# A local transformer inside a gated cross-attention stack: round and layer loops written out, weight parts sent in earlier rounds

## The chip, the cores and the metric

The program runs on one core of one Trainium2 chip. The core's engines are TensorE (PE; its weight loads are shown apart, as PEld), VectorE (DVE), ScalarE (ACT), GpSimd (POOL) and SyncE (SP, which issues the DMAs here). The metric is the device time of one execution in microseconds (us); lower is better.

## The reference, cut to what matters

An activation of 16 sequences x 128 tokens x 128 channels passes four gated cross-attentions, each followed by a gated feed-forward network. The first of these networks is a local transformer of its own, six layers deep. It takes two thirds of the time and is what the change touches:

```python
for i in range(DEPTH):      # 6 layers
    x = attn_layer(shift_tokens(x), Wqkv[i], q_scale[i], k_scale[i], Wo[i]) + x
    x = ffn_layer(shift_tokens(x), ln_g[i], ln_b[i], W1[i], b1[i], W2[i], b2[i]) + x

# attn_layer: 16 heads of 64 channels; l2-normalised and rotated queries and keys;
# each token sees its own window of 32 tokens and the one before it
# ffn_layer: layer norm, 128 -> 2 x 341 channels, a * gelu(gate), 341 -> 128
```

## The kernel before

A unit is one sequence (128 tokens) in one layer, so the local transformer has 6 x 16 = 96 units. The units are pipelined four deep. In round n every engine works on part `a` of unit n, part `b` of unit n-1, part `c` of unit n-2 and part `d` of unit n-3. `stages(a, b, c, d)` is one round; each engine has its own, with its instructions in an order written out by hand, and the engines meet through semaphores alone. Layer l's unit n follows layer l-1's unit 15 without a pause, so in a layer's first three rounds some parts still belong to the layer before. There are two sets of buffers for units (`s`, the unit's parity) and two sets of layer weights (`lw[p]`, `qk_scale[p]`, with p the parity of the layer). The first PE instruction of a round is the transpose in `tokens_T`, line L860; the times of rounds below are cut at its starts.

`local_transformer` drives PE, ACT, DVE and POOL. For each layer it writes out rounds 0 to 3, runs rounds 4 to 13 in a hardware loop of five trips with two rounds in each (L515), and writes out rounds 14 and 15. Layer 0 comes first, then a hardware loop of two trips (L525), each with an odd and an even layer (1 and 2, then 3 and 4), then layer 5. In a loop, the count that an instruction waits for is worked out in registers. In rounds 14 and 15 of layers 0 to 4, PE multiplies the next layer's value and output weights together (`values_outputs`, matmuls L1002, which read `wvT` and `wout` in the buffer `moe1_gu` and count `l_wvo_ps`), and POOL makes the next layer's rotary tables ahead of round 14.

SP is driven by `layer_and_next_weights`: its rounds within a layer were written out already, its layer pairs are a loop (L618). Its `stages` issues, in this order:

```python
if c: middle_values0(*c)              # L583: 4 DMAs, after ACT has copied the values; PE needs them a round later
if d: shifted_tokens(*d)              # L595: 1 DMA, after DVE's first residual (l_y1, L2274); DVE's L2278 waits for it
if c: middle_values1(*c, edge=edge)   # L591: 4 DMAs
```

A unit's `c` and `d` on SP belong to work that the other engines do as `a`, `b` and `c`: SP's stage n runs during the others' round n-1. Behind its stage SP sends weights for layers to come: four value parts (256 KB each, to `wvT` and `wout`) and, in layers 1 to 4, eight layer parts (`wqk`, the feed-forward weights, columns, scales) into the other set of `lw`. One part goes behind each stage, beginning with n = 3. Ahead of the first stand two waits: for `l_wvo_ps` (the products that read `wvT` and `wout`), and for `ffn_done`, the count of second residuals (DVE, L2308), which says that the last unit of the layer before is through, so that its weights can be written over.

Of the kernel before, what the change touches and what calls it, by code (L numbers as in the profile page):

```python
# [23 lines left out]
IT = B // G  # L24
DEPTH, LH, LD = 6, 16, 64
# [48 lines left out]
def program(nc, dram, out):  # L74
# [6 lines left out]
    with ctx:  # L81
# [409 lines left out]
        def layer_unit(p, lp, n):  # L491

            if n >= 0:
                return (n % G, At(p, lp, n // G))
            if p:
                return (n % G, At(0, lp, IT + n // G))
            return None if isinstance(lp, int) and lp == 0 else (n % G, At(1, lp - 1, IT + n // G))

        def local_transformer(engine, stages, prepare=None, fresh=False, drain=None):

            def rounds(p, lp, lo, hi, last=True):
                for n in range(lo, hi):
                    four = (layer_unit(p, lp, n - k) for k in range(4))
                    if fresh and not last:
                        stages(*four, fresh=(1 - p, lp + p, n - lo))
                    else:  # L510
                        stages(*four)

            def layer(p, lp, last):
                rounds(p, lp, 0, 4)
                with engine.Fori(2, IT - 1) as pr:  # L515
                    stages((0, At(p, lp, pr)), (1, At(p, lp, pr - 1)), (0, At(p, lp, pr - 1)), (1, At(p, lp, pr - 2)))
                    stages((1, At(p, lp, pr)), (0, At(p, lp, pr)), (1, At(p, lp, pr - 1)), (0, At(p, lp, pr - 1)))
                if prepare and not last:
                    prepare(1 - p, lp + p)
                rounds(p, lp, B - G, B, last)  # L520

            if prepare:
                prepare(0, 0)
            layer(0, 0, False)
            with engine.Fori(0, DEPTH // 2 - 1) as lp:  # L525
                layer(1, lp, False)
                layer(0, lp + 1, False)
            layer(1, DEPTH // 2 - 1, True)
            for n in range(B, B + 3):
                stages(*(layer_unit(1, DEPTH // 2 - 1, n - k) if n - k < B else None for k in range(4)))  # L530
                if drain and n == B + 1: drain()
# [5 lines left out]
        def _(sp):  # L537
# [14 lines left out]
            def layer_parts(p, l):  # L552

                rows = dram["wqk"][l, :, :]
                parts = [[(wqk[p][:, at:at + 512], rows[:, at:at + 512])] for at in range(0, 2 * INNER, 512)]
                parts += [
                    [(wff1[p], dram["wff1"][l, :, :])],
                    [(wff2[p][:, 0:2, :], dram["wff2"][l, 0:256, :].rearrange("(c p) n -> p c n", p=128)),
                     (wff2[p][0:HID - 256, 2, :], dram["wff2"][l, 256:HID, :])],
                    [(lcol[p][:, :], dram["lcol"][l, :, :]), (bff2[p], dram["bff2"][bass.ds(l, 1), :].partition_broadcast(S))],  # L560
                    [(qk_scale[p][:, 0, :], dram["q_scale"][bass.ds(l, 1), :].partition_broadcast(S)),
                     (qk_scale[p][:, 1, :], dram["k_scale"][bass.ds(l, 1), :].partition_broadcast(S))],
                ]
                return parts

            def value_parts(l):

                return [(dst[:, c:c + 4, :], dram[name][l, :, c:c + 4, :]) for dst, name in ((wvT, "wvT"), (wout, "wout")) for c in (0, 4)]
# [28 lines left out]
            def stages(a, b, c, d):  # L597
                edge = a is None or d is None
                if c: middle_values0(*c)
                if d: shifted_tokens(*d)  # L600
                if c: middle_values1(*c, edge=edge)

            def layer_and_next_weights(p, lp, fresh):

                parts = [[(part, wv_loaded)] for part in value_parts(2 * lp + p + 1)]
                if fresh:
                    parts += [[(move, lw_loaded[1 - p]) for move in part] for part in layer_parts(1 - p, 2 * lp + p + 1)]
                for n in range(B):
                    stages(*(layer_unit(p, lp, n - k) for k in range(4)))
                    if n == 3:  # L610
                        sp.wait_ge(l_wvo_ps, 2 * (2 * lp + p + 1))
                        sp.wait_ge(ffn_done, G + (2 * lp + p) * B)
                    if 3 <= n < 3 + len(parts):
                        for (dst, src), done in parts[n - 3]:
                            sp.dma_start(dst, src).then_inc(done, 16)

            layer_and_next_weights(0, 0, False)
            with sp.Fori(0, DEPTH // 2 - 1) as lp:  # L618
                layer_and_next_weights(1, lp, True)
                layer_and_next_weights(0, lp + 1, True)  # L620
            for n in range(B + 3):
# [64 lines left out]
        def _(pe):  # L686
# [556 lines left out]
            for half in range(2):  # L1243
                values_outputs(0, 0, half)
            pe.wait_ge(t_prep, 1)
            local_transformer(pe, stages, fresh=True, drain=first_value_rows)
            attention(XA[1])
            pe.wait_ge(w1_loaded, 128)
# [10 lines left out]
        def _(act):  # L1259
# [376 lines left out]
            for half in range(2):  # L1636
                values_outputs(0, 0, half)
            local_transformer(act, stages, fresh=True, drain=first_value_rows)
            act.wait_ge(w1_loaded, 112)
            attention(XA[1])  # L1640
# [9 lines left out]
        def _(pool):  # L1650
# [241 lines left out]
            for s in range(G):  # L1892
                pool.wait_ge(x_updated, G + LNY)
                pool.memset(xsT[s][:, 0:1], 0.0)
                pool.memset(ysh[s][:, D:D + 64], 0.0).then_inc(v_ones, 1)
            quad_inverse_stds([3])
            local_transformer(pool, stages, rotary_factors)
            attention(XA[1])
            for q in range(QUADS):
# [764 lines left out]
```

## Time and profile before

| | before |
|---|---|
| median of 3 runs | 2504.11 us (2498.87 to 2506.43) |
| profiled execution | 2502.32 us, span 2500.4 us |
| PE busy | 2379.8 us, 95% of the span |
| DVE, ACT, POOL busy | 1861.0, 1770.3, 1662.9 us (74%, 71%, 67%) |
| local transformer, rounds 0 to 95 | 131.5 to some 1767.5 us |
| mean granted PE clock | 0.981 |

A timeline row gives the start, the time taken, engine, line, operation, output and inputs, the number of instructions merged into it, and in brackets the engine's idle time just before it with what ended it. SPq and PEldq are instructions of the sequencer of SP and of PE: issues, register work, branches. A row of a stretch gives its bounds and length, each engine's busy time with its number of instructions, the granted PE clock (1.00 is 2.4 GHz), the DMA share and the GB/s moved. "issue" stands for a wait that no semaphore of the profile explains.

### The profile page before, as it was taken

Reading aid. Unit: us, or ns where it says so; the run is one execution under the profiler, and the core shown is the slowest. Engines: PE = TensorE matmul, PEld = TensorE weight load, DVE = VectorE, ACT = ScalarE, POOL = GpSimd, SP = SyncE. Lnnn points to the kernel's source line nnn. Section 1 sums busy time; section 2 is a strip of 40 time slices with the busy share of each in tenths; the row PEclk is TensorE's granted clock in tenths of the full one; section 3 lists DMA queues with packets and bytes.
Section 4 is the critical chain, followed back from the end, with each engine's and each line's share of the span. In section 5 each row is a group of like instructions: output and inputs, shape, how many; then the busy total and the mean of one; then the engine's idle time right before and its main releaser. Section 6 shows DMA issues by size and latency. Waiting matters only on the chain. (4 is left out here: it accounts for less than half of the span.)

```text
span 2500.4 us, 84963 instructions
## 1 busy us (share of the span) xinstructions
PE 2379.8 (95%) x32650; PEld 1666.1 (67%) x32650; DVE 1861.0 (74%) x4616; ACT 1770.3 (71%) x3859; POOL 1662.9 (67%) x2011
## 2 busy tenths in 40 slices
PE   8889999999999999999999999999889898999898
PEld 6746666566666666566666666666468777999567
DVE  6768887888878887788778878888387776555574
ACT  5668888888878887888878888888653375332555
POOL 5668888888888887788888888888341164000562
PEclk9989999999999999999999999999999998999899
DMA  3011111121111111221121112111350000000022
GB/s 132 2 36 41 34 33 37 48 52 46 32 48 50 47 36 33 55 54 36 34 55 44 48 36 53 33 32 37 89 172 1 1 2 1 1 0 1 20 68 84
DMA packets 98410, 104.07 MB, mean 42 GB/s; under 512 B 34873, under 2 KB 60548, under 8 KB 97540
## 3 DMA queue, kind: packets, MB, share of 16 engines
q1 hardware_dynamic: 98180, 100.93, 15.2%
q8 instruction: 154, 2.52, 0.4%
q14 instruction: 76, 0.62, 0.1%
HBM read 41.31 MB, written 6.09 MB: 19 GB/s over the span
## 5 line engine op out<-in xcount | busy, mean ns | idle before, releaser
L1261 ACT ACTIVATE area<-ps 64x128 f32<-64x128 f32 (+7 forms) x1480 | 747.0, 530 | 201.2 <-PE ps L860 64.8
L1761 POOL TENSOR_TENSOR area<-area 128x512 f32<-128x512 f32 x384 | 485.7, 1275 | 128.5 <-DVE area L2239 120.9
L1776 POOL TENSOR_TENSOR area<-area,rnq 128x512 f32<-128x512 f32 x384 | 397.2, 1045 | 15.3 <-ACT rnq L1434 8.3
L870 PE MATMUL ps<-lw,area 128*128 128x512 f32 x768 | 375.4, 611 | 4.5 <-DVE area L2239 3.2
L898 PE MATMUL ps<-lw,area 128*64 128x512 f32 x1536 | 373.0, 606 | 0.1
L2237 DVE TENSOR_TENSOR area<-ps,table 128x512 f32<-128x512 f32 x384 | 261.3, 681 | 16.9 <-ACT area L1398 16.8
L2219 DVE TENSOR_REDUCE ssq<-area 128x8 f32<-128x512 f32 x384 | 259.6, 676 | 2.1 <-ACT area L1398 2.1
L2239 DVE TENSOR_TENSOR area<-ps,table 128x512 f32<-128x512 f32 x384 | 259.9, 677 | 0.0
L887 PE MATMUL ps<-ident,area 128*128 128x128 f32 x1536 | 237.7, 278 | 5.0 <-POOL area L1776 4.8
L1398 ACT ACTIVATE area<-ps 128x512 f32<-128x512 f32 x384 | 216.8, 590 | 29.3 <-PE ps L870 29.2
L887 PEld LDWEIGHTS ps<-ident,area 128*128 128x128 f32 x1536 | 178.7, 141 | 78.3 <-issue 57.0
L1528 ACT ACTIVATE area<-ps 128x256 f32<-128x256 f32 x208 | 79.2, 384 | 202.2 <-PE ps L1074 202.1
L953 PEld LDWEIGHTS ps<-area 128*32 128x32 f32 x6144 | 156.2, 110 | 90.6 <-issue 63.3
L1784 POOL TENSOR_TENSOR area<-area,mx 128x512 f32<-128x512 f32 x192 | 200.3, 1043 | 22.1 <-DVE mx L2256 21.4
L953 PE MATMUL ps<-area 128*32 128x128 f32 x6144 | 207.9, 276 | 1.5 <-ACT area L1261 1.5
L870 PEld LDWEIGHTS ps<-lw,area 128*128 128x128 f32 x768 | 131.4, 191 | 108.9 <-issue 93.7
L1792 POOL TENSOR_TENSOR area<-area,rc 128x512 f32<-128x512 f32 x192 | 200.0, 1042 | 2.6 <-DVE rc L2270 2.4
L925 PEld LDWEIGHTS ps<-area 64*32 64x32 f32 x12288 | 134.0, 105 | 90.6 <-issue 79.3
L898 PEld LDWEIGHTS ps<-lw,area 128*64 128x64 f32 x1536 | 92.9, 136 | 144.1 <-issue 111.0
L971 PEld LDWEIGHTS ps<-xnT,lw 128*128 128x128 f32 (+1 forms) x1152 | 147.1, 182 | 47.0 <-issue 45.0
L925 PE MATMUL ps<-area 64*32 64x64 f32 x12288 | 164.9, 224 | 1.6 <-ACT area L1261 1.6
L971 PE MATMUL ps<-xnT,lw 128*128 128x128 f32 (+1 forms) x1152 | 162.4, 278 | 0.6 <-ACT xnT L1261 0.6
(290 smaller groups left out, 4950.9 us busy)
## 6 DMA issues: line engine op xcount, KB each, us to landing
area<-area SPq DMA_DIRECT2D x768, 64.0 KB, 2.0
lw<-in_wqk SPq DMA_DIRECT2D x24, 256.0 KB
area<-in_moe_w SPq DMA_DIRECT2D x24, 256.0 KB, 2.8
area<-product_rows SPq DMA_DIRECT2D x16, 256.0 KB
moe_gu<-in_wvT SPq DMA_DIRECT2D x12, 256.0 KB, 3.0
moe_gu<-in_wout SPq DMA_DIRECT2D x12, 256.0 KB, 3.0
area<-area SPq DMA_DIRECT2D x96, 31.8 KB
product_rows<-lw SPq DMA_DIRECT2D x7, 308.0 KB
```

Source lines behind the costliest of these rows:

```text
L870: nc.tensor.matmul(banks[:, lb_qk[j], :], xsT[s], wqk[w.p][:, j * 512:(j + 1) * 512], start=True, stop=True).then_inc(l_qk_ps, 1)
L887: last = nc.tensor.transpose(banks[:, lb_qkT[j], c * S:(c + 1) * S], QR[s][:, j * 512 + c * 128:j * 512 + (c + 1) * 128], ident[:, :])
L898: last = nc.tensor.matmul(banks[64 * odd:64 * odd + 64, lb_v[j], :].rearrange("p (c n) -> p c n", n=D), xsT[s][:, 64 * near:64 * near + 64 ...
L925: last = nc.tensor.matmul(banks[out_rows, lb_scores[m][odd], c * 64:(c + 1) * 64].rearrange("p (b n) -> p b n", n=WINDOW), QKT[s][64 * odd ...
L953: last = nc.tensor.matmul(banks[32 * n:32 * n + 32, lb_att, 0:D], LPT[s][:, at:at + 32], v, start=(c == 0), stop=(c == 7))
L971: last = nc.tensor.matmul(banks[0:hi - lo, lb_up[value], c * S:(c + 1) * S], wff1[w.p][:, at:at + hi - lo], xnT[s][:, :], start=True, stop ...
L1261: return nc.scalar.activation(dst, src, ACT.Identity if kw else ACT.Copy, **kw)
L1761: pool.tensor_tensor(QR[s][:, cols], QR[s][:, cols], RA[s][:, cols], ALU.add).then_inc(l_rsum, 1)
L1776: pool.tensor_tensor(rows, rows, rnq[s][:, 8 * j:8 * j + 8, None].to_broadcast([S, 8, LD]), ALU.mult).then_inc(l_qkn, 1)
L2219: V.tensor_reduce(ssq[s][:, 8 * j:8 * j + 8], blk(SQ[s], j), AX.X, ALU.add).then_inc(l_ss, 1)
L2237: V.tensor_tensor(blk(RA[s], j), src, factors[:, 0:1, :].to_broadcast([S, 8, LD]), ALU.mult)
L2239: V.tensor_tensor(blk(QR[s], j).rearrange("p h (k e) -> p h k e", k=2), other, factors[:, 1:2, :].to_broadcast([S, 8, LD]).rearrange("p h ...
```

## The change

Two things change, with no arithmetic touched. First, all hardware loops of `local_transformer` and SP's loop over layer pairs become Python loops: the 96 rounds (and the three that drain the pipeline) stand one after the other in each engine's program, and every wait is for a constant. Second, SP begins to send parts behind stage 0 instead of stage 3. The wait for `l_wvo_ps` goes with it to n = 0; the wait for `ffn_done` stands at n = 4, ahead of the first layer part.

```diff
             def layer(p, lp, last):
                 rounds(p, lp, 0, 4)
-                with engine.Fori(2, IT - 1) as pr:
+                for pr in range(2, IT - 1):
                     stages((0, At(p, lp, pr)), (1, At(p, lp, pr - 1)), (0, At(p, lp, pr - 1)), (1, At(p, lp, pr - 2)))
                     stages((1, At(p, lp, pr)), (0, At(p, lp, pr)), (1, At(p, lp, pr - 1)), (0, At(p, lp, pr - 1)))
...
             layer(0, 0, False)
-            with engine.Fori(0, DEPTH // 2 - 1) as lp:
+            for lp in range(DEPTH // 2 - 1):
                 layer(1, lp, False)
                 layer(0, lp + 1, False)
...
                 for n in range(B):
                     stages(*(layer_unit(p, lp, n - k) for k in range(4)))
-                    if n == 3:
+                    if n == 0:
                         sp.wait_ge(l_wvo_ps, 2 * (2 * lp + p + 1))
+                    if n == 4:
                         sp.wait_ge(ffn_done, G + (2 * lp + p) * B)
-                    if 3 <= n < 3 + len(parts):
-                        for (dst, src), done in parts[n - 3]:
+                    if n < len(parts):
+                        for (dst, src), done in parts[n]:
                             sp.dma_start(dst, src).then_inc(done, 16)
 
             layer_and_next_weights(0, 0, False)
-            with sp.Fori(0, DEPTH // 2 - 1) as lp:
+            for lp in range(DEPTH // 2 - 1):
                 layer_and_next_weights(1, lp, True)
                 layer_and_next_weights(0, lp + 1, True)
```

## Rows read from the trace of the kernel before

**Rows 1.** Busy time by stretch: the local transformer whole, with the columns.
```profile
core 0: us, PE busy (x) PEld busy (x) DVE busy (x) ACT busy (x) POOL busy (x), PEclk, DMA share, GB/s
131.50:1767.50 1636.00, 1600.69 (x25034) 1003.55 (x25036) 1312.97 (x2962) 1340.46 (x2798) 1367.46 (x1466) 1.00 0.17 42
```

**Rows 2.** Busy time by stretch: round 3 of layers 0 to 5, one row each.
```profile
182.30:198.74 16.44, 16.44 (x265) 10.35 (x260) 13.62 (x31) 13.86 (x29) 14.51 (x16) 1.00 0.20 52
451.14:470.41 19.27, 16.74 (x266) 10.29 (x261) 13.63 (x31) 13.86 (x29) 14.22 (x16) 1.00 0.26 68
723.14:741.77 18.63, 16.73 (x265) 10.28 (x260) 13.64 (x31) 13.87 (x29) 14.20 (x16) 1.00 0.26 70
999.61:1019.11 19.50, 16.80 (x266) 10.34 (x261) 13.63 (x31) 13.91 (x29) 14.20 (x16) 1.00 0.26 66
1271.81:1290.44 18.63, 16.74 (x267) 10.28 (x261) 13.64 (x31) 13.86 (x29) 14.22 (x16) 1.00 0.26 70
1542.98:1559.41 16.43, 16.43 (x265) 10.36 (x260) 13.59 (x31) 13.86 (x29) 14.20 (x16) 1.00 0.15 36
```

**Rows 3.** Timeline of PE in round 3 of layer 1, its two idle times.
```profile
458.66 1.12 PE L870 MATMUL ps<-lw,area 128*128 128x512 f32 x2 [1.08 <-DVE area L2239]
...
461.90 0.66 PE L939 MATMUL ps<-ident,area 128*128 128x128 f32 x4 [1.45 <-POOL area L1792]
```

**Rows 4.** Timeline of DVE at the start of that round.
```profile
449.19 0.29 DVE L2308 TENSOR_TENSOR Y<-ps,area 128x128 f32<-128x128 f32 x1 [0.19 <-PE ps L985]
...
456.78 0.29 DVE L2278 BATCH_NORM_STATS2 st<-area 128x6 f32<-128x128 f32 x1 [4.12 <-DMA area<-area]
```

**Rows 5.** Timeline of SP's issues, stages 3 and 4 of layer 1.
```profile
434.49 2.77 SPq L591 DMA_DIRECT2D area<-area  x4
449.67 0.38 SPq L615 DMA_DIRECT2D moe_gu<-in_wvT  x1
450.21 3.01 SPq L583 DMA_DIRECT2D area<-area  x4
453.35 0.66 SPq L595 DMA_DIRECT2D area<-area  x1
```

**Rows 6.** Waits of SP's queue over the whole span: total, times, longest.
```profile
SPq L615 <- DVE Y L2308: 48.2, 4, 12.1
```

**Rows 7.** Timeline of SP's issues, stages 0 and 1 of layer 1.
```profile
383.68 2.86 SPq L591 DMA_DIRECT2D area<-area  x4
395.77 2.41 SPq L583 DMA_DIRECT2D area<-area  x4
```

**Rows 8.** Timeline of PE in round 15 of layer 0.
```profile
392.07 1.16 PE L1002 MATMUL ps<-moe_gu 64*128 64x128 f32 x16
```

**Rows 9.** Busy time by stretch: rounds 15 and 0, layers 0/1, then 2/3.
```profile
383.58:401.09 17.51, 17.51 (x282) 11.31 (x277) 13.59 (x31) 14.84 (x31) 14.23 (x16) 1.00 0.15 35
401.09:417.92 16.83, 16.53 (x266) 10.42 (x260) 13.67 (x31) 13.86 (x29) 13.87 (x16) 1.00 0.15 35
926.90:948.68 21.78, 17.64 (x283) 11.32 (x277) 15.80 (x33) 14.85 (x31) 16.11 (x18) 0.99 0.15 35
948.68:966.39 17.71, 17.71 (x260) 11.68 (x260) 12.52 (x29) 13.74 (x29) 11.75 (x14) 0.91 0.12 29
```

**Rows 10.** Instructions of line L525 (outer loop): duration min/median/max in ns.
```profile
L525 PEldq COMPARE_BRANCH  x2: 76/2116/4157, 944.3 to 1493.0; - x2
```

**Rows 11.** Instructions of line L515 (inner loop), the same columns.
```profile
L515 PEldq COMPARE_BRANCH  x30: 76/208/242, 231.9 to 1725.3; - x30
```

**Rows 12.** Busy time by stretch: rounds 1-2 of layers 1, 5; rounds 4-13 of 5.
```profile
417.92:451.14 33.22, 32.93 (x526) 20.73 (x520) 27.26 (x62) 27.72 (x58) 28.41 (x31) 1.00 0.13 31
1509.84:1542.98 33.14, 32.90 (x526) 20.73 (x522) 27.18 (x62) 27.72 (x58) 28.40 (x31) 1.00 0.25 68
1559.41:1725.47 166.06, 165.14 (x2607) 104.03 (x2600) 136.27 (x310) 138.62 (x290) 141.99 (x151) 1.00 0.14 34
```

**Rows 13.** DMA queues of the page: kind, packets, MB, share of 16 engines.
```profile
q8 instruction: 154, 2.52, 0.4%
```

## The prediction

> **What bounds the kernel now.** I began with the share of busy time: over the local transformer PE works 1600.7 of 1636.0 us, 98% [rows 1]. DVE, ACT and POOL have about a sixth of their time free. So the pace is PE's, and what can be won here without taking matmuls away is at most PE's idle time of 35.3 us plus whatever stretches its matmuls. I then cut the stretch at the first PE instruction of each round, which gives 96 rounds to compare. An undisturbed round takes 16.4 to 16.8 us, odd and even ones in turn: layer 5's round 3 takes 16.43 us with PE busy throughout [rows 2]. The rounds that stand out are few: round 3 of layers 1 to 4 [rows 2], the step between the two trips of the outer loop [rows 9], and rounds 13 to 15 of layers 0 to 4, which do extra work (rotary tables on POOL, 16 extra matmuls on PE [rows 8]) that the change leaves where it is.
>
> **Round 3.** Layers 1 to 4 take 19.27, 18.63, 19.50 and 18.63 us there, layer 0 takes 16.44 and layer 5 16.43 [rows 2]. The number of instructions on each engine is the same; what is added is idle time, on PE 1.08 us behind DVE and 1.45 us behind POOL [rows 3]. Going backwards: DVE stood 4.12 us waiting for the shift DMA [rows 4]. SP issued that DMA (L595) at 453.35 us. It had ended stage 3 at 437.26 us and issued nothing until 449.67 us, 0.2 us after the second residual of DVE (449.19 + 0.29) [rows 4, 5]; in the queue's own list of waits it is the weight part that waited for L2308, 4 times, 48.2 us [rows 6]. Queued behind this wait were the weight part, four value copies (L583, 3.01 us of issuing) and then the shift. The value copies could have been issued in the 12 us of standstill. So the `ffn_done` wait at n = 3 delays the shift by about the 3.7 us from 449.67 to 453.35 us. It happens in exactly the four layers that have a previous layer to wait for.
>
> With the change SP meets this wait at n = 4, behind the shift DMA of stage 4. That DMA itself waits for DVE's first residual of round 3 (L2274), which stands behind the second residual of round 2 in DVE's own order. When SP comes to the new wait it is therefore satisfied and holds nothing back. The first DMA behind it is a layer part, 0.38 us of issue, in a place where parts stood before. I expect all four rounds to fall to layer 5's 16.43: 2.84 + 2.20 + 3.07 + 2.20 = 10.3 us. The ends of the range: 0 if something else then arrives last, 10.3 if nothing does. I take 10.3.
>
> **The wait moved to n = 0.** `l_wvo_ps` is counted by the matmuls L1002 in round 15, which end at 393.23 us [rows 8]. SP has ended stage 0 at 386.54 and its next issue is at 395.77 us, held by ACT's copy [rows 7]. The wait ends 2.5 us ahead of that, and a part takes 0.38 us to issue [rows 5]. So nothing behind it is issued late: not the value copies of stage 1, nor the shift behind those. The 256 KB then move ahead of the copies. If the copies land 3 us later for it (the size of the queue's whole delay above), PE still needs them only in the middle of the next round, some 12 us after. Cost 0, cover more than 9 us. Parts 1 to 3 and the eight layer parts go behind stages 1 to 11, places equal to those that stages 4 to 14 had. The last part lands some three rounds earlier; POOL's tables before round 14 did not wait for it before, so no gain.
>
> **The outer loop.** Rounds 15 and 0 take 17.51 + 16.83 = 34.34 us between layers 0 and 1, and 21.78 + 17.71 = 39.49 us where the outer loop branches back [rows 9]. The branch on PE's sequencer took 4157 ns there and 76 ns where it falls through [rows 10]. The second part of the loss is 0.9 us in the round after: no PE idle, but the granted clock has a mean of 0.91, that is, part of it at 1.2 instead of 2.4 GHz, after an idle of 4.1 us. Written out, both go: 39.49 - 34.34 = 5.15 us. DVE, ACT and POOL lose less at their own branches and are not the pace. The Trainium skill has this rule in "Runtime: NRT & Kernel Launch", section "Instruction fetch mechanics": a taken branch to a page that is not in the instruction buffer waits for a DMA fetch. The trace agrees, with 4157 ns.
>
> **The inner loops.** Of 30 branches on PE, 24 are taken, at some 208 ns each [rows 11]. If each showed in full on PE the gain would be 24 x 0.208 = 5.0 us. But PE's idle time is no larger in the loop: layer 5 is busy 165.14 of 166.06 us over ten loop rounds, idle 0.92, and busy 32.90 of 33.14 in two written ones, idle 0.24, or 1.20 for ten [rows 12]. The branch only takes the place of a wait for POOL that the written rounds have. What is left is the difference of the totals: 166.06 - 5 x 33.14 = 0.36 us a layer, 2.2 us for six. Written rounds of layers 1 to 4 still use registers for the layer: 33.22 for two rounds against 33.14 in layer 5 [rows 12]. With rounds 0 and 3 alike that is 0.16 us a layer, 0.6 us for four. Sum 2.8, bounds 0 and 5.0 + 0.6 = 5.6.
>
> The Trainium skill puts a compare-and-branch at some 108 ns ("Advanced Engine Details and Errata", section "Control Flow Timing"). The trace has nearly twice that on PE [rows 11]; by the page 24 branches would be an estimated 2.6 us.
>
> **What is added: a longer program.** Written out, the body is 99 rounds of instructions instead of 4 x 8 + 3 = 35. PE runs some 526 matmuls in two rounds [rows 12], as many weight loads, and 24 repeated trips were served without a new fetch: 24 x 2 x 526 = 25,200 instructions. Its queue brought 154 packets, 2.52 MB, so 16.4 KB each [rows 13]; PE's other 40,000 instructions over 154 packets are some 260 a packet. That makes about 97 more packets. Do they cost time? Layer 5's rounds 1 to 3 are written out, are fetched as they run, and are the fastest of all; round 3 has no PE idle at all [rows 2, 12]. So 0; the bound above follows with the rivals.
>
> **Sum.** 10.3 + 5.15 + 2.8 = 18.3 us, 0.7%. The profiled execution's span of 2500.4 becomes 2482.1, and its own time 2502.3 becomes 2484.0. It lay 1.8 us below the median of the runs, 2504.1, so I predict a median of 2485.8, rounded to 2486. About 0.3%, 7.5 us, can be told from no change.
>
> **Rivals.**
> (a) *The shift stays late.* If the four slow rounds came from the weight part itself, its 256 KB ahead of the shift in the queue, or if the stall moved to round 4, only the loops would be won: 2504.1 - 8.0 = 2496. For it: round 3 is the first with a part. Against it: rounds 4 and on have parts of the same size and normal times, and layer 0 sends its first part at n = 3 too, has no earlier layer to wait for, and takes 16.44 us [rows 2]. Chance 0.05. If besides this the loops brought only the outer branch, it would be 2499, within 0.3%.
> (b) *Fetching becomes the bound.* Straight code must be fetched at PE's pace for all 96 rounds beside the weight parts. If each of the 97 added packets cost one short branch, 0.208 us, that is 20.2 us and eats the gain: 2506, no change. From (18.3 + 7.5) / 97 = 0.27 us a packet the kernel is slower. The same could happen on DVE, ACT or POOL. Against it: the written rounds are no slower than the looped ones anywhere in these rows [rows 2, 12]. Chance of no change 0.03, of slower 0.02. The same page of the Trainium skill, in the same section, has sequential fetches as mostly hidden; the rows say so for six rounds in a row, not for 96.
> (c) *The branches do count.* The POOL wait of 0.24 us in two rounds could vanish as well, once POOL has no register work, so that the written loops win the whole 5.6 instead of 2.8, and up to 0.24 in each of 48 pairs: 11.5 us. Layer 5's written rounds have hardly register work and still wait. With 5.6 the time is 2483. With the POOL wait gone too it is some 2473. Chance 0.10, most of it near 2483.
> (d) *Later loops lie badly.* All code behind moves; a loop whose body lay within the buffer could straddle it. The mixture's loops have 4 taken branches on PE; at 4.2 us each, 2486 becomes 2503. Chance 0.02.
>
> **How the numbers follow.** Forecast 0.78, (a) 0.05, (b) 0.05, (c) 0.10, (d) 0.02. The forecast's own range is 2482 to 2490: the small terms by 3 us, the median of three runs by some 3. To hold eight in ten and part of (c) and (a), 2480 to 2493. Faster 0.93; same: 0.03 of (b), 0.01 of (a) and (d), so 0.04; slower 0.03.
>
> **What the profile after would show.** Round 3 of layers 1 to 4 at 16.4 us, DVE's longest wait at L2278 there near the others', no row "SPq L615 <- DVE Y". The first value part of layer 1 issued near 393.3 us on today's scale, with the copies behind it at their old time. Rounds 15 and 0 between layers 2 and 3 at 34.3 us at a full clock. No compare-and-branch in the local transformer. The instruction queue near 250 packets, 4.1 MB. Pairs of rounds at 33.1 us. I would be wrong if PE idles behind "issue" in straight code, if the shift stays late in any round, or if the time behind the local transformer (733 us now) changes by more than 2 us.

## The result and the profile after

The changed kernel takes 2479.19 us (median of four runs, 2475.41 to 2480.79), the kernel before 2505.21 on the same chip. The ratio is 0.9899, 95% interval 0.9879 to 0.9919: faster by some 25 us, where 18.3 were forecast (2486 us, range 2480 to 2493). The four runs of the kernel before were on the high side: against 22 runs of it in a later session (median 2500.42) the changed kernel's repeat is 22.9 us faster. The profiled execution took 2479.18 us with a span of 2477.3, against 2502.32 and 2500.4. PE was busy for 2368.2 us of it, and of the queues of the page those that bring instructions grew, q8 as the forecast had it (154 packets before [rows 13]):

```profile
q8 instruction: 249, 4.08, 0.7%
q14 instruction: 88, 0.72, 0.1%
```

Busy time by stretch, the changed kernel: the local transformer from the first to the last start of a round; round 3 of layers 1 and 2; rounds 15 and 0 between layers 2 and 3; rounds 1-2 of layers 1 and 5; rounds 4-13 of layer 5.

```profile
131.64:1724.73 1593.09, 1571.42 (x24662) 985.17 (x24660) 1290.40 (x2918) 1321.43 (x2758) 1349.08 (x1443) 1.00 0.18 44
450.51:466.94 16.43, 16.43 (x265) 10.36 (x261) 13.59 (x31) 13.87 (x29) 14.22 (x16) 1.00 0.20 52
719.61:736.04 16.43, 16.43 (x281) 10.37 (x273) 13.60 (x32) 13.88 (x30) 14.21 (x16) 1.00 0.20 52
...
921.38:938.90 17.52, 17.52 (x282) 11.31 (x277) 13.59 (x31) 14.85 (x31) 14.26 (x16) 1.00 0.19 49
938.90:955.64 16.74, 16.48 (x267) 10.37 (x262) 13.60 (x31) 13.87 (x29) 13.90 (x16) 1.00 0.20 51
417.28:450.51 33.23, 32.91 (x526) 20.73 (x522) 27.18 (x62) 27.75 (x58) 28.42 (x31) 1.00 0.21 52
1492.79:1525.91 33.12, 32.88 (x526) 20.73 (x522) 27.19 (x62) 27.74 (x58) 28.42 (x31) 1.00 0.24 68
1542.34:1708.04 165.70, 164.45 (x2607) 103.69 (x2602) 135.97 (x310) 138.73 (x290) 142.05 (x151) 1.00 0.15 36
```

Cut in the same way, the kernel before had 1610.7 us from the first start of a round to the last. So 17.6 of the 23.1 us by which the two spans differ lie in the local transformer, with round 3 at 16.43 us where it was 18.63 to 19.50 [rows 2] and the outer loop's step at 34.26 instead of 39.49 [rows 9]. The other 5.6 lie behind the start of its last round, in code that nobody touched. The same view there, first the kernel before: to the hardware loop of the last cross-attention ("the last loop" below), over its start, over its five full trips, to the end.

```profile
1742.18:2266.76 524.58, 480.34 (x4615) 415.27 (x4610) 344.58 (x1037) 255.06 (x569) 146.34 (x250) 0.96 0.11 32
2266.76:2366.07 99.31, 90.06 (x733) 75.98 (x732) 53.02 (x163) 38.97 (x100) 30.09 (x59) 0.91 0.02 7
2366.07:2449.67 83.60, 75.42 (x682) 55.17 (x682) 57.97 (x210) 50.72 (x141) 57.99 (x111) 1.00 0.24 73
2449.67:2500.38 50.71, 43.33 (x357) 39.82 (x356) 20.81 (x81) 24.72 (x86) 5.90 (x12) 0.90 0.25 81
```

And the changed kernel, with the same instructions in each stretch:

```profile
1724.73:2248.66 523.93, 480.39 (x4615) 415.37 (x4610) 344.66 (x1039) 255.10 (x569) 146.54 (x250) 0.96 0.11 32
2248.66:2344.23 95.57, 86.08 (x733) 73.46 (x732) 52.70 (x162) 39.02 (x100) 30.20 (x59) 0.96 0.02 7
2344.23:2426.51 82.28, 75.42 (x682) 55.13 (x682) 57.01 (x210) 50.68 (x141) 58.17 (x111) 1.00 0.25 74
2426.51:2477.27 50.76, 43.42 (x357) 40.40 (x356) 20.71 (x81) 24.84 (x86) 5.92 (x12) 0.90 0.25 81
```

Two different things stand in them. Over the start, 3.74 us: PE is busy 3.98 us less with the same 733 matmuls, at a granted clock of 0.96 instead of 0.91, so less of the stretch ran at 1.2 GHz. Over the five trips, 1.32 us: PE is busy the same 75.42 us at a full clock, and a trip takes 16.45 instead of 16.67 to 16.72.

The queue of SP did what was forecast. Its timeline at the end of layer 0 and in stages 3 and 4 of layer 1:

```profile
392.72 0.34 SPq L616 DMA_DIRECT2D moe_gu<-in_wvT  x1
395.21 2.42 SPq L583 DMA_DIRECT2D area<-area  x4
...
436.30 0.59 SPq L616 DMA_DIRECT2D moe_gu<-in_wout  x1
445.30 3.16 SPq L583 DMA_DIRECT2D area<-area  x4
449.92 0.66 SPq L595 DMA_DIRECT2D area<-area  x1
450.61 2.78 SPq L591 DMA_DIRECT2D area<-area  x4
453.43 0.58 SPq L616 DMA_DIRECT2D lw<-in_wqk  x1
```

The value copies of stage 4 no longer stand behind a part that waits, and the shift goes out at 449.92. On DVE the instruction that needs it follows at 453.34 after 1.31 us of waiting, where it had stood 4.12 us [rows 4]:

```profile
453.34 0.30 DVE L2279 BATCH_NORM_STATS2 st<-area 128x6 f32<-128x128 f32 x1 [1.31 <-DMA area<-area]
```

### The profile page after: what moved, and what is told of

Read it like the earlier page. It is cut to its first block and busy times, and to the rows that moved or that the text cites. A ratio compares the mean times of both kernels' runs of the same rounds, so it can differ in the third digit from the quotient of the medians.

```text
span 2477.3 us, 81251 instructions
## 1 busy us (share of the span) xinstructions
PE 2368.2 (96%) x32650; PEld 1660.2 (67%) x32650; DVE 1855.6 (75%) x4616; ACT 1772.0 (72%) x3859; POOL 1665.1 (67%) x2011
```

## The experiments

"Local" below is the time from the first to the last start of a round, "tail" what follows, both from the profiled execution. The kernel before has 1610.7 and 758.2, the changed one 1593.1 and 752.5. Ratios are against the kernel before.

**e1: the loops alone.** All three loops written out, SP's parts and waits as before.

```diff
-                with engine.Fori(2, IT - 1) as pr:
+                for pr in range(2, IT - 1):
...
-            with engine.Fori(0, DEPTH // 2 - 1) as lp:
+            for lp in range(DEPTH // 2 - 1):
...
-            with sp.Fori(0, DEPTH // 2 - 1) as lp:
+            for lp in range(DEPTH // 2 - 1):
```

> The loops are written out, SP sends its parts as before (from n = 3, both waits there). Theory A (the local transformer's gain is the sum of the late shift, the outer branch and the written rounds; the rest of the gain lies behind it and is the granted clock there): from the first to the last round start 8 us less than before, that is 1603 us; round 3 of layers 1 to 4 still at 18.6 to 19.5 us. Rival B (the late shift comes from the loops, not from the wait): round 3 falls to 16.4 us and the stretch to 1593 us. The stretch behind the last round start (758.2 us before, 752.5 after): under A either value, depending on the clock granted near the start of the last attention; under B2 (written loops shorten it) 752.5.

Measured: 2486.15 us, ratio 0.9934 (0.9918 to 0.9951); local 1602.2, tail 751.8. The local part gained 8.5 us, where 8.0 were forecast for the loops. Round 3 of layers 1 to 4 stayed slow, at 18.3, 19.3, 18.3 and 19.0 us; together that is 1.1 us less than before, which is part of the 8.5.

**e2: the parts and waits alone.** SP's parts and waits as changed, all loops kept.

```diff
-                    if n == 3:
+                    if n == 0:
                         sp.wait_ge(l_wvo_ps, 2 * (2 * lp + p + 1))
+                    if n == 4:
                         sp.wait_ge(ffn_done, G + (2 * lp + p) * B)
-                    if 3 <= n < 3 + len(parts):
-                        for (dst, src), done in parts[n - 3]:
+                    if n < len(parts):
+                        for (dst, src), done in parts[n]:
```

> The loops stay, SP sends its parts from n = 0 with the ffn_done wait at n = 4. Theory A: round 3 of layers 1 to 4 at 16.4 us, the stretch of round starts 10.3 us less than before, 1600.4 us; the outer branch still costs 4 us on PE. Rival (the weight part, not the wait, makes the shift late): round 3 stays near 19 us, or another round takes the stall over. Whole time by A 2494 to 2495 us, or some 5 us less if the clock stays up near the start of the last attention.

Measured: 2493.32 us, ratio 0.9956 (0.9941 to 0.997); local 1601.0, tail 760.2. Busy time by stretch: round 3 of layer 1, then rounds 15 and 0 between layers 2 and 3.

```profile
451.40:467.89 16.49, 16.47 (x267) 10.37 (x261) 13.64 (x31) 13.86 (x29) 14.21 (x16) 1.00 0.20 53
922.30:944.28 21.98, 17.64 (x282) 11.32 (x277) 15.81 (x33) 14.86 (x31) 16.26 (x18) 1.00 0.19 48
944.28:962.29 18.01, 18.01 (x261) 11.51 (x262) 12.59 (x29) 13.91 (x29) 11.60 (x13) 0.91 0.17 43
```

Round 3 is repaired and the outer step is not. Local, the halves gain 8.5 and 9.7 us, together 18.2, against 17.6 for both at once: they add up to within 0.6 us. The tail shrank with e1 and not with e2, in one profile each.

**e3: the wait back at n = 3, the parts early.** From the changed kernel, as e4.

```diff
-                    if n == 4:
+                    if n == 3:
                         sp.wait_ge(ffn_done, G + (2 * lp + p) * B)
```

> The changed kernel with one edit: the ffn_done wait stands at n = 3 again (ahead of the last value part), parts still go from n = 0. Theory A: the wait alone makes the loss, round 3 of layers 1 to 4 at 18.6 to 19.5 us again and the stretch of round starts 10 us above that of the changed kernel, 1603 us. Rival (the order of parts or their number makes it): 1593 us as in the changed kernel.

Measured: 2487.29 us, ratio 0.9936 (0.992 to 0.9953); local 1602.1, tail 752.3. Round 3 of layer 1:

```profile
451.28:469.53 18.25, 16.74 (x266) 10.28 (x261) 13.59 (x31) 13.86 (x29) 14.21 (x16) 1.00 0.26 69
```

The others took 18.25, 19.20 and 19.45. One wait moved by one stage costs 9.0 us. In stage 3 the part behind it is here an output-weight part whose buffer had long been free, so the wait itself does the harm.

**e4: the parts from n = 3 again, the wait ahead of the first layer part (n = 7).**

```diff
-                    if n == 0:
+                    if n == 3:
                         sp.wait_ge(l_wvo_ps, 2 * (2 * lp + p + 1))
-                    if n == 4:
+                    if n == 7:
                         sp.wait_ge(ffn_done, G + (2 * lp + p) * B)
-                    if n < len(parts):
-                        for (dst, src), done in parts[n]:
+                    if 3 <= n < 3 + len(parts):
+                        for (dst, src), done in parts[n - 3]:
```

> The changed kernel with the parts sent from n = 3 as before, and the ffn_done wait at n = 7, ahead of the first layer part. Theory A: no stall anywhere, the stretch of round starts 1593 us, so that the earlier start of the parts is worth nothing by itself. Rival (a part ahead of the shift in the queue is late enough to hurt): round 3 above 17 us.

Measured: 2480.30 us, ratio 0.9913 (0.9897 to 0.993); local 1592.6, tail 749.7, round 3 at 16.45 us. Locally this is the changed kernel to 0.5 us. Sending parts three rounds earlier is worth nothing by itself; that the wait left n = 3 is worth all of it.

**e5 and e6: one loop level at a time.** From the kernel before, e5 writes out the outer loop and SP's (the second and third of the three edits of e1), e6 the inner loop alone (the first).

> Only the outer loop of the four engines and SP's loop are written out; the inner loops of rounds 4 to 13 stay, SP's parts as before. In the local transformer: 5.1 us less than before (no 4.2 us branch on PE, no slow round behind it), 1605.6 us from the first to the last round start. Behind it: if the written code as such makes the faster steady state of the last attention (trips of 16.45 instead of 16.66 us) then this kernel has it or not according to where its instruction pages begin; if the shorter local transformer made it, it should be there only with the full change.

> Only the inner loops are written out; the outer loop and SP's loop stay. In the local transformer 2 to 3 us less than before, 1608 us: the outer branch still costs 4.2 us and a slow round behind it. If instead the outer branch cost only what it cost because of the inner loops (page order), round 15 of layer 2 falls to 17.5 us.

Measured: e5 2492.86 us, ratio 0.997 (0.9958 to 0.9981), local 1606.8, tail 750.4; e6 2500.79 us, ratio 0.9998 (0.9989 to 1.0008), local 1616.1, tail 753.8. In e5 rounds 15 and 0 between layers 2 and 3 took 17.50 and 16.75 us, so the branch is gone; but round 3 of layer 1 rose from 19.27 to 19.83 and that of layer 2 from 18.63 to 19.38, and the local part gained 3.9. The last loop's trips took 16.44 us in e5 and 16.54 in e6. In e6's profile the local part lost 5.4. Round 3 of layer 1 there, and rounds 15 and 0:

```profile
450.88:473.15 22.27, 19.57 (x266) 11.49 (x261) 13.63 (x31) 13.97 (x29) 14.55 (x16) 0.85 0.22 57
929.86:952.45 22.59, 17.63 (x283) 11.33 (x277) 16.10 (x33) 14.89 (x31) 16.26 (x18) 0.98 0.16 38
952.45:971.63 19.18, 19.18 (x261) 12.17 (x262) 12.78 (x29) 14.00 (x29) 11.64 (x13) 0.84 0.10 24
```

The outer step is 41.77 us here, 2.3 more than before [rows 9], and PE ran part of two rounds at 1.2 GHz. Not all of this belongs to the edit. Rounds 4 to 13 of the six layers gained 1.0 us together (2.0 in e1). The branch back took 4.97 us on PE's sequencer, against 3.87 to 4.42 in the seven profiles that have the outer loop and all inner ones. But the low clock behind the branch varies with these loops kept as well (the round after it takes 17.7 us before, 19.0 in e17), and so does the one in round 3 of layer 1 (a granted clock of 0.92 in e12, 1.00 in the other six, 0.85 here). Ten runs of e6 take as long as the kernel before. So written-out inner loops inside an outer loop bring nothing; a loss of 5.4 us is not shown.

**e7 and e8: both kernels once more, unchanged.**

> The changed kernel once more, for a second profile. From the first to the last round start 1593 us again, to 0.5 us: that part is fixed by the program. Behind it: trips of the last attention 16.45 us again if the program fixes them; the granted clock at its start may be at 2.4 or 1.2 GHz, so 752 to 757 us, if that is chance; always 752.5 if the program fixes it.

> The kernel before once more, for a second profile. From the first to the last round start 1610.7 us again; trips of the last attention 16.66 us; behind the last round start 758 us if the low clock at the start of the last attention (10.2 us at 1.2 GHz) belongs to the program, down to 753 us if it is chance. Whole time within 0.2% of before.

Measured: the changed kernel 2477.54 us, ratio 0.9901 (0.9884 to 0.9919), local 1592.7, tail 751.6; the kernel before 2501.82 us, 1.0004 (0.9994 to 1.0014), local 1611.9, tail 759.2. The local parts differ by 19.2 us in this pair, 1.3 of them in round 1 of layer 0. The difference behind the last round is there again, 7.6 us. But it lies elsewhere. The changed kernel's repeat, by the four stretches shown above:

```profile
1724.98:2246.26 521.28, 476.05 (x4614) 411.33 (x4610) 344.51 (x1039) 255.04 (x569) 146.30 (x250) 0.97 0.11 33
2246.26:2345.59 99.33, 90.08 (x733) 76.03 (x732) 52.79 (x162) 39.19 (x100) 30.10 (x59) 0.91 0.02 7
2345.59:2427.81 82.22, 75.41 (x682) 55.14 (x682) 56.99 (x210) 50.66 (x141) 58.01 (x111) 1.00 0.24 73
2427.81:2476.56 48.75, 41.01 (x357) 37.87 (x356) 20.70 (x81) 24.67 (x86) 5.90 (x12) 0.96 0.27 84
```

The 3.7 us over the start of the loop are lost again, and 2.6 and 2.0 us are won in the first and last stretch, each with the clock. Only the 1.3 us of the five trips repeat to 0.1 us: they belong to the program. The rest goes with the granted clock, whose low stretches move from one execution to the next.

**e10 and e15: the changed kernel with its DVE code moved.** Both add 32 tiny memsets at the start of DVE, so that its later instructions stand 32 places further on. e10 writes them to a new buffer, which also moves the buffers behind it; e15 to one that is there.

```diff
+        pad = sb("pad", [S, 32])                       # e10
...
+            for k in range(32):
+                V.memset(pad[:, k:k + 1], 0.0)         # e10
+                V.memset(sm[k // 16][:, k % 16:k % 16 + 1], 0.0)   # e15 instead
```

> The changed kernel with 32 tiny memsets on a spare tile at DVE's start, so that every later DVE instruction lies 32 places further on in its pages. Theory (the 0.3 us stops of DVE near a page fetch are page crossings): rounds 5 of layer 1 and 11 and 0 of layer 2, now 16.8 and 17.1 us, move to other rounds or vanish. Theory T (such a stop at the start of the last attention, 0.37 us, brings on its trips of 16.45 us): trips go back to 16.66 us. Rival: trips stay 16.45 us, then written code or the time of arrival makes them.

> The changed kernel with 32 tiny memsets at DVE's start on tiles that exist, so no buffer moves and only DVE's instructions move in their pages. Page theory: the long rounds (0 and 11 of layer 2, 5 of layer 1) move or vanish while every other round keeps its 16.43 or 16.74 us; the trips of the last attention leave 16.45 us if a page step at its start sets them. Rival (pages do nothing): all as in the changed kernel.

Measured: e10 2479.35 us, ratio 0.9914 (0.9896 to 0.9932), local 1592.6, tail 751.8; e15 2480.97 us, 0.9917 (0.99 to 0.9934), local 1593.3, tail 755.9. A trip of the last loop took 16.55 and 16.54 us instead of 16.45, where the first expectation had 16.66. At the start of that loop, DVE in the changed kernel and in the kernel before:

```profile
2324.12 0.18 DVE L2485 BATCH_NORM_AGGREGATE e_mv<-e_st 128x2 f32<-128x6 f32 x1 [0.37 <-issue]
```

```profile
2345.63 0.18 DVE L2484 BATCH_NORM_AGGREGATE e_mv<-e_st 128x2 f32<-128x6 f32 x1
```

In the changed kernel DVE stands 0.37 us at this instruction, once, and for nothing that the trace names. With the code moved by 32 places the stop is not there, and the trips are 0.1 us longer. But the stop is not what makes them short: e5 has none here, and its trips take 16.44. The long trips go with another stop, 22.8 us further on. The kernel before there, then e5 at the same instruction:

```profile
2368.40 0.75 DVE L2436 SCALAR_TENSOR_TENSOR area<-ps,q_rs,small 128x512 f32<-128x512 f32 x1 [0.25 <-issue]
```

```profile
2361.19 0.72 DVE L2436 SCALAR_TENSOR_TENSOR area<-ps,q_rs,small 128x512 f32<-128x512 f32 x1
```

Of the 19 profiles four have this stop: the kernel before, its repeat, e2 and e14. They are the four whose trips settle at 16.66 to 16.67 us; the others settle at 16.44 to 16.56. No run takes this one stop away by itself, so that it makes the long trips is likely and not shown.

**e11, e12, e14 and e17: the kernel before with one small thing added.** e11 adds a buffer of 4 bytes a partition and one reduction into it (0.25 us of DVE) at the start of the last loop; e14 the buffer alone; e17 the reduction alone, into a buffer that is there; e12 the 32 memsets of e10 with their buffer.

```diff
+        spare = sb("spare", [S, 1])                                   # e11, e14
...
+                    if isinstance(it, int) and (s, it) == (0, 0):
+                        V.tensor_reduce(spare[:, :], X[:, 0, :], AX.X, ALU.add)      # e11
+                        V.tensor_reduce(w_mv[:, 0:1], X[:, 0, :], AX.X, ALU.add)     # e17
```

> The kernel before with one more DVE instruction, once (0.3 us, a reduction of X to a spare column), at the place of the last attention where DVE stops for 0.37 us in the changed kernel. Theory T: trips of the last attention fall from 16.66 to 16.45 us, so the stretch behind the last round start is 1 us shorter. Rival: 16.66 us stay, and the stretch is 0.3 us longer or equal.

> The kernel before with the same 32 tiny memsets at DVE's start. Local transformer 1611 us as before. If instruction pages alone decide the trips of the last attention, they may change from 16.66 us here; under the rival they stay. If the granted clock behind the local transformer (72.7 to 72.8 us at 1.2 GHz in two profiles of before, 52 to 64 in those with a loop written out) goes with the trips or the pages, it changes too; if it is chance it lies anywhere between 52 and 76.

> The kernel before with the spare tile alone, without the extra DVE instruction. Theory A2: the stretch of round starts is 1600.5 us as with the instruction, against 1610.7 us. Trips of the last attention 16.55 us if the place of the buffers makes them (three kernels with moved buffers had 16.55), 16.66 us if the extra instruction did. Rival: 1610.7 us, everything came from the instruction.

> The kernel before with one more DVE instruction, once, in the last attention, on a tile that exists, so that no buffer moves. Theory (the steady state of the last attention is set by DVE's timing at its start): trips fall from 16.66 to 16.55 us as in the run that had the instruction and a moved buffer, and the local transformer stays at 1611 us. Rival (only moved buffers or written loops change it): trips 16.66 us, stretch behind the last round start 758 to 759 us as in both profiles of before.

| | us, ratio (95%) | local | tail | trip |
|---|---|---|---|---|
| e11 | 2489.29, 0.9955 (0.9942 to 0.9969) | 1600.5 | 751.7 | 16.56 |
| e12 | 2503.85, 1.0011 (1.0001 to 1.0021) | 1617.1 | 751.4 | 16.56 |
| e14 | 2491.93, 0.9963 (0.9949 to 0.9976) | 1601.6 | 755.9 | 16.67 |
| e17 | 2502.09, 0.9995 (0.9986 to 1.0004) | 1612.0 | 758.9 | 16.54 |

One 0.25 us instruction on DVE shortens the trips by 0.11 us (e11 against e14, e17 against before). It doesn't shorten the tail by itself: e17 has short trips and 758.9 us. So a trip's length depends on how DVE stands to the other engines near the start of the loop. And an unused buffer of 4 bytes a partition is worth 9 us in the local transformer, which I had not looked for; e11's gain there was the buffer's, not the reduction's. That led to the next run.

**e13: the changed kernel with the unused buffer.**

```diff
+        spare = sb("spare", [S, 1])
```

> The changed kernel with a spare tile of 4 bytes a partition allocated ahead of most others and never used; no instruction changes, all later buffers move. Theory A2 (in the kernel before, with such a tile and one extra instruction, the shift DMA landed 0.3 us earlier in every other round, and the wait of PE for POOL in those rounds went): the stretch of round starts falls from 1592.9 to 1582 to 1584 us, all undisturbed rounds at 16.4 us. Rival (the extra instruction or the loops had to do with it): 1592.9 us stay.

Measured: 2464.49 us, ratio 0.9857 (0.9839 to 0.9875), where the changed kernel had 0.9899 and 0.9901, so 11 us by the ratios; local 1578.8, 14 less, tail 749.8. DVE's wait for the shift in round 0 of layer 1, in the changed kernel and then in e13:

```profile
403.68 0.29 DVE L2279 BATCH_NORM_STATS2 st<-area 128x6 f32<-128x128 f32 x1 [1.63 <-DMA area<-area]
```

```profile
401.38 0.29 DVE L2280 BATCH_NORM_STATS2 st<-area 128x6 f32<-128x128 f32 x1 [1.32 <-DMA area<-area]
```

In even rounds the shift landed 0.3 us later than in odd ones (medians 1.62 and 1.31 us of wait); with the buffers moved both take 1.32. SP issues it at the same point, 0.6 us ahead of the round. The 0.3 us went by way of POOL to PE, as the idle time of its transposes shows (grouped lines of PE in the local transformer, the changed kernel, then e13):

```profile
L940 PE MATMUL ps<-ident,area 128*128 128x128 f32 x752 | 118.6, 280 | 14.5 <-POOL area L1793 13.9
```

```profile
L941 PE MATMUL ps<-ident,area 128*128 128x128 f32 x752 | 118.5, 280 | 2.0 <-POOL area L1794 1.3
```

That is 12.6 us of PE's idle time, and two written rounds (1-2 of layer 1) now take 32.88 us, PE without a pause:

```profile
414.97:447.85 32.88, 32.88 (x526) 20.73 (x521) 27.19 (x62) 27.75 (x58) 28.45 (x31) 1.00 0.20 52
```

In e12 the pad moved the late landing to the odd rounds (waits of 1.31 in even and 1.62 us in odd ones), and the local part grew to 1617.1; in e10 it moved as well (1.31 and 1.63), with 1592.6.

**e9 and e16: the rotary tables spread.** Round 13 of layers 0 to 4 takes 17.4 us in the changed kernel, because POOL multiplies all factors of the next layer's tables at once. In e9 it does two of the six in each of rounds 12, 13 and 14, ahead of its rotary sums; e16 is e9 with e13's buffer.

```diff
+                    if prepare and not last and pr == IT - 2:
+                        prepare(1 - p, lp + p)
...
-                    pool.tensor_tensor(table[p][:, i, 0, :], qk_scale[p][:, i, :], rot[:, 2 * i, :], ALU.mult)
+                    factors_left.append((table[p][:, i, 0, :], qk_scale[p][:, i, :], rot[:, 2 * i, :]))
...
+            def some_factors(count):
+                for k in range(min(count, len(factors_left))):
+                    dst, scales, factors = factors_left.pop(0)
+                    op = pool.tensor_tensor(dst, scales, factors, ALU.mult)
+                    if not factors_left:
+                        op.then_inc(tables_ready, 1)
...
+                some_factors(2)
```

> The changed kernel with one more edit: the six small POOL instructions that make the next layer's rotary tables no longer stand in one piece ahead of round 14, but two each in rounds 12, 13 and 14, in the place where POOL waits for DVE. They can, since the scales now land three rounds earlier. Theory (the six in a row, 1.6 us on POOL, lengthen round 13 from 16.4 to 17.4 us in five layers): round 13 back near 16.5 us and 3 to 5 us less in all. Rival (round 13 is long by its position in the pipeline, or the small instructions push POOL's chain wherever they stand): no gain, 0 to 2 us.

> The changed kernel with the tables spread over rounds 12 to 14 and the spare tile. If the two gains are independent, the stretch of round starts is 1588.6 - 10 = 1578 to 1579 us and the time 2463 to 2467 us; if the tables' place only paid because of the wait for POOL in every other round, it is near that of the changed kernel with the spare tile alone.

Measured: e9 2474.59 us, ratio 0.9892 (0.9874 to 0.991), local 1588.6; e16 2458.22 us, ratio 0.9826 (0.9808 to 0.9844), local 1574.7, the fastest of all. Over e13 the spread tables gain 4.0 us locally, over the changed kernel 4.5: the two gains add up. Round 13 of layer 0, the changed kernel, then e9:

```profile
347.80:365.20 17.40, 17.00 (x265) 10.44 (x261) 14.74 (x31) 13.76 (x29) 15.35 (x22) 1.00 0.15 35
```

```profile
348.50:364.91 16.41, 16.41 (x267) 10.36 (x260) 13.59 (x31) 13.87 (x29) 14.68 (x18) 1.00 0.16 37
```

## Why the prediction was right and where it was not

**Round 3 (10.3 us): right, and shown.** All four rounds fell to 16.43 or 16.44. e3 gives 9.0 us of it back by the wait alone, e2 gains 9.7 without any loop touched, e4 has the gain with the parts where they were. Rival (a), that the part rather than the wait makes the shift late, falls.

**The wait at n = 0 (0 us): right.** The first part went out at 392.72 us, in SP's gap, and the copies behind it 2.5 us later as before.

**The outer loop (5.15 us): right in the whole, 5.23 measured.** The repeated pair has 6.1, for a lower clock behind the branch in the repeat of the kernel before. Alone it gives 3.9 (e5): the step itself is 5.2 shorter there, and round 3, where the wait still stands, took 0.6 of it back over the four layers.

**The inner loops and registers (2.8 us): right in the whole, 2.1 measured** (17.6 less 10.3 and 5.23). Rounds 4 to 13 gained 1.9 us of the 2.2 forecast for them. The 0.6 us for registers are not seen where they were put: rounds 1 and 2 of layer 1 took 33.22 us before and 33.23 after. The pairs were at 33.12 to 33.23 us, so the waits for POOL stayed, against rival (c). Its price of 11.5 us for them was near: e13 removes 12.6 us of them, by the place of a buffer and not by code. (Its last figure should be 2471.5 us, 2485.8 less 2.8 and 11.5, and not 2473.)

**The longer program (0 us, rival (b) up to 20): nearly right.** PE never waits for code, with 249 packets. The stops are DVE's, and they are small. One of them, and what it does to PE 4 us later:

```profile
487.37 0.69 DVE L2238 TENSOR_TENSOR area<-ps,table 128x512 f32<-128x512 f32 x1 [0.27 <-issue]
```

```profile
491.96 0.65 PE L940 MATMUL ps<-ident,area 128*128 128x128 f32 x4 [0.33 <-POOL area L1793]
```

Two such stops stand in the local part, 385 DVE instructions apart, its queue's included (487.37 and 673.54 us), and an 8 KB packet of q14 follows 0.7 and 1.1 us behind. A third, at 856.21 us, shows as a wait of 0.46 us for DVE's own result where 0.10 is usual. The three rounds that they stand in are 0.35 us longer, 1.1 us in all, and so they are in the repeat. In e15, with DVE's code moved by 32 places, all three fell into rounds of layers 3 and 4. The Trainium skill, "Runtime: NRT & Kernel Launch", section "Instruction fetch mechanics", has the step from one block to the next as mostly hidden. The trace agrees for PE; on DVE the 0.27 us may be such a step, since the stops move with the code.

**What failed.** It is the step that put the change of the time behind the local transformer at nothing: the sum has no term for it and gives no reason, the last section allows it 2 us, and only rival (d) has it move, at 0.02 and the other way. The local terms came to 17.6 us for 18.3 forecast; the time from the last start of a round to the end fell by 5.6 in one pair of profiles and 7.6 in the other. Rival (d)'s far branches did not come about either: PE's six branches there take 76 to 215 ns before and 76 to 247 after. The fall has two parts.

The first is shown in the main: 1.3 us are the five full trips of the last loop. That their length hangs on how DVE stands to the other engines there is shown, by e11 and e17 with one instruction of DVE; what moved it from 16.66 to 16.45 us in the changed kernel is likely the missing stop at L2436.

The second is not settled: the other 4 to 6 us go with the granted clock. Behind the last start of a round the kernel before, its repeat and e2 spent 71.7 to 75.1 us at 1.2 GHz, the changed kernel, its repeat, e1, e3 and e4 54.6 to 61.7. A straight line through the 19 profiles gives 0.39 us of tail for each of these us (an estimate, correlation 0.91), so 3.9 for the 10 by which the first pair differs. It isn't the loops as such: the kernel before with a moved buffer (e11, e12, e14) had 54.9 to 61.4 and e5, with its inner loops, 51.2, while e15, with all loops written out, had 68.3 and a tail of 755.9. The trips' length doesn't decide it (e17: 16.55 us, and 78.5 at the low clock), and neither does any one stretch (e7 loses 3.7 us over the loop's start and wins them elsewhere). Nor is it an accident of two profiles: the mean granted clock of a whole execution was 0.982 over 68 runs of the kernel before and 0.984 over eight of the changed one. Why the mean differs stays open.

## What to carry to other kernels

A wait at the head of a queue costs whatever is queued behind it; move it behind the transfers that the current round needs, and look first at who is held up, not at the bytes. A loop level written out alone may bring nothing: inner loops written out in a looped outer one left the time as it was here, with a branch back of 4.97 us. A forecast that adds up local terms is good for its stretch, and should leave several us for the tail of a kernel whose clock or whose trips depend on when each engine arrives.

## What the runs showed of the hardware that I had not expected

- An unused buffer of 4 bytes a partition, ahead of others, made a DMA between buffers land 0.3 us earlier in every second round: 14 us of the local part in the changed kernel, 9 in the one before. Which property of the addresses does it was not tried.
- In straight code DVE stopped for some 0.3 us at three points of the local part, each with an 8 KB packet of q14 some 1 us behind, and the points moved with DVE's code. PE was never seen to stop there, while q8 brought 249 packets of 16 KB.
- The last loop's trip settled at some 16.45, 16.55 or 16.66 us with the same instructions and PE busy the same 75.4 us in five trips; a single 0.25 us instruction of DVE took it from 16.66 to 16.55.
- PE's far branch took 3.9 to 4.4 us in seven profiles with all loops kept, and 4.97 in the one with the inner loops written out (e6). In the round after it PE runs part of the time at 1.2 GHz (a mean granted clock of 0.84 to 0.92).
